# A ViT tower's fusion convolutions: the last 64 channels of both image halves in one 128-partition tile

## The reference

```
dwconv(x, wd, wp, bp): y = depthwise 3x3 (pad 1) of x with wd;  return 1x1 conv of y with wp, + bp
loc  = dwconv(gelu(patch_conv(x)), pl_dw, pl_pw, pl_pwb)
g    = gelu(dwconv(gelu(conv1x1(wavelet_packet(x))), pg_dw, pg_pw, pg_pwb))
glob = conv1x1(g, pg_w2, pg_b2)
h = (1 - gate) * loc + gate * glob              # gate = 0.5 * (tanh(alpha) + 1), per channel
h = relu(dwconv(h, f1)); h = relu(dwconv(h, f2)); h = dwconv(loc + h, f3)
tokens = layernorm(h over the 192 channels) * ln_g + ln_b, and a class token
```

## Time and profile before

| | us |
|---|---|
| median of 3 runs | 229.34 (228.66 to 230.13) |
| profiled execution | 229.1 |
| its span | 227.2 |
| mean granted TensorE clock | 0.852 |

### The profile page before, as it was taken

The page is one execution under the profiler, slowest core; times in us unless marked ns, Lnnn a source line. Parts: engine busy times, 40 slices in busy tenths (PEclk is TensorE's granted clock), DMA queues, the critical chain, the costliest instruction groups (busy, mean ns, idle before and its releaser), DMA issues.

```text
span 227.2 us, 2861 instructions
## 1 busy us (share of the span) xinstructions
PE 161.9 (71%) x928; PEld 133.6 (59%) x928; DVE 102.2 (45%) x302; ACT 47.6 (21%) x89; POOL 75.2 (33%) x196
## 2 busy tenths in 40 slices
PE   0999998888888827610212999999999999993000
PEld 0677754455555415610102899999999999992000
DVE  1129994998899494472103122222332222203445
ACT  0353344343111203210000111232111231110000
POOL 1799300000000121027668877882000000004761
PEclk9999999999999965555555699999999999997555
DMA  6990499999990000003265001000000000011222
GB/s 217 331 408 13 116 265 261 250 261 257 272 341 22 0 1 0 0 0 117 82 197 186 0 5 33 18 19 20 17 31 24 17 20 17 17 38 44 77 56 80
DMA packets 14932, 23.46 MB, mean 103 GB/s; under 512 B 1599, under 2 KB 11396, under 8 KB 14790
## 3 DMA queue, kind: packets, MB, share of 16 engines
q1 hardware_dynamic: 12800, 19.80, 29.9%
q0 software_dynamic: 928, 2.09, 3.0%
q10 hardware_dynamic: 1190, 1.38, 1.9%
HBM read 17.96 MB, written 5.31 MB: 102 GB/s over the span
## 4 chain that ended last, share of the span: by engine, by line
PE 65%; DVE 11%; issue 9%; POOL 5%; DVEq 4%; DMA 3%; ACT 1%; POOLq 0%
PE ps L965 20%; PE ps L975 14%; PE ps L814 8%; PE ps L822 7%; PE ps L823 5%; PE ps L868 4%; POOL diag_s L398 4%; DVEq L746 4%; PE ps L802 3%; DMA w1t_s<-in_w1t 2%; DVE conv L570 1%; DVE stats L616 1%; DVE conv L582 1%; POOL rstd L378 1%; DVE zt L647 1%
## 5 line engine op out<-in xcount | busy, mean ns | idle before, releaser
L965 PE MATMUL ps<-conv 128*128 128x128 f32 x384 | 48.2, 285 | 6.9 <-DVE conv L751 6.5
L965 PEld LDWEIGHTS ps<-conv 128*128 128x128 f32 x384 | 47.3, 201 | 7.6 <-issue 6.8
L570 DVE SCALAR_TENSOR_TENSOR conv<-conv,vecs 128x240 f32<-128x240 f32 (+1 forms) x94 | 35.9, 444 | 7.3 <-ACT conv L447 6.8
L975 PE MATMUL ps<-w_s,conv 128*128 x192 | 33.7, 326 | 0.0
L760 DVE COPY arena<-ps 128x192 f32<-128x192 f32 x16 | 5.7, 358 | 57.5 <-PE ps L975 57.5
L975 PEld LDWEIGHTS ps<-w_s,conv 128*128 128x128 f32 x192 | 30.9, 190 | 0.0
L398 POOL DMA_INDIRECT diag_s<-slot_results,slots x10 | 9.6, 961 | 54.9 <-DMA slot_results<-arena 52.1
L378 POOL TENSOR_TENSOR rstd<-var,neghalf 128x2 f32<-128x2 f32 (+1 forms) x6 | 4.8, 807 | 62.9 <-DVE var L622 62.9
L507 ACT COPY conv<-ps 128x256 f32<-128x256 f32 x16 | 6.0, 373 | 82.8 <-PE ps L956 82.8
L751 DVE COPY conv<-w_s 128x1536 f32 x16 | 15.2, 957 | 14.5 <-issue 9.5
L822 PE MATMUL ps<-conv,pw_s 128*128 128x288 f32 (+1 forms) x48 | 17.4, 445 | 5.5 <-DVE conv L582 3.8
(11 more groups left out here) (152 smaller groups left out, 185.8 us busy)
## 6 DMA issues: line engine op xcount, KB each, us to landing
w_s<-in_w SPq DMA_DIRECT2D x8, 576.0 KB, 18.1
w_s<-in_w SPq DMA_DIRECT2D x8, 384.0 KB
slot_rows<-zero SPq DMA_DIRECT2D x1, 2048.0 KB, 22.2
arena<-in_x SPq DMA_DIRECT2D x4, 432.0 KB, 9.6
w_s<-in_w SPq DMA_DIRECT2D x8, 192.0 KB
slot_results<-arena SPq DMA_DIRECT2D x16, 96.0 KB, 1.6
pw_s<-in_pw SPq DMA_DIRECT2D x1, 1152.0 KB, 11.5
arena<-slot_rows SPq DMA_DIRECT2D x1, 1024.0 KB, 7.6
```

The costliest lines, as they stand in the source:

```text
L570: ins = nc.vector.scalar_tensor_tensor(out=o, in0=a, scalar=w, in1=o, op0=ALU.mult, op1=ALU.add)
L965: last = mm(p1_ps[i % 2][:, c * P:(c + 1) * P], w1_cur[:, i % 2, k * F + c * P:k * F + (c + 1) * P], xs[:, i % 2, k * P:(k + 1) * P], star ...
L975: last = mm(y_ps[i % 2], hT[:, i % 2, k * P:(k + 1) * P], w2_flat[:, bass.ds(expert[i] * (FK * D) + k * D, D)], start=(k == 0), stop=(k == ...
```

## The change

- A fusion round no longer has four tiles but three units: (g 0, t 0), a packed tile (t 1) with half 0 on partitions 0 to 63 and half 1 on 64 to 127, and (g 1, t 0). VectorE, and TensorE with its tap sums, do the units one after another. In round 0 the packed tile is done as two units, its lower and its upper half.
- To get half 1's last channels onto the upper partitions, branches(1) writes its output parts to the swapped halves. The 1x1 weights of tile 1 exist in a second version, pwx, with the rows on the other 64 partitions and zeros on the rest, loaded by one more DMA of 384 KB. A zero fill on POOL clears the part of loc that meets zero weights.
- In rounds 1 and 2 TensorE makes the three upper taps of all three units; in round 0 those of the upper half of the packed tile and of (g 1, t 0). The order of TensorE's queue is new.
- Each fusion 1x1 makes its 64-channel part first. The branches' last pair waits for the third output, not the fourth.
- The constant row is computed after fusion(0, 1), into bank 7, and copied after it.

```diff
-PE_HELPS = [(0, 1), (1, 0), (1, 1), (2, 0), (2, 1)]
+UNITS = [(0, 0), (0, 1), (1, 0)]
+UNIT_BANK = (2, 3, 6)
+FIRST_UNITS = [(0, 0, slice(0, P), 5), (1, 0, slice(0, DB), 6), (1, 1, slice(DB, P), 12), (2, 1, slice(0, P), 12)]
+PE_HELPS = [(0, 1), (0, 2), (1, 0), (1, 1), (1, 2), (2, 0), (2, 1), (2, 2)]
...
# SP
             sp.dma_start(pw_s[:], pw).then_inc(d_pw, 16)
+            sp.dma_start(pwx_s[:], pwx).then_inc(d_pwx, 16)
             sp.dma_start(layout_s[:], layout).then_inc(d_misc, 16)
...
# POOL, ahead of the diagonals
+            nc.gpsimd.memset(loc[LO, 1, HPX:NPX], 0.0).then_inc(loc_zero, 1)
...
# ScalarE
             def branches(g):
+                own, other = (LO, HI) if g == 0 else (HI, LO)
+                first, second = px(0), px(1)
...
-                evacuate(n + 2, b + 1, loc[HI, 1, px(g)], HI, ACT.Gelu, vcol("bias2", 1, HI))
+                evacuate(n + 2, b + 1, loc[other, 1, second], other, ACT.Gelu, vcol(bias, k, other))
...
             def fusion(f, g):
-                evacuate(n + 1, b, act_a[:, 0, px(g)], A, fn, vcol("fb", 2 * f))
-                evacuate(n + 2, b + 1, act_a[LO, 1, px(g)], LO, fn, vcol("fb", 2 * f + 1, LO))
+                if f == 2:
+                    evacuate(n + 1, b + 1, act_a[LO, 1, px(g)], LO, fn, vcol("fb", 2 * f + 1, LO))
+                else:
+                    own = LO if g == 0 else HI
+                    evacuate(n + 1, b + 1, act_a[own, 1, px(0)], own, fn, vcol("fb", 2 * f + 1, own))
+                if f == 0 and g == 1:
+                    act.wait_ge(pw_ev, n + 1)
+                    middle_tap(0, 1, A, V["dwf"] + 18, 1)
+                evacuate(n + 2, b, act_a[:, 0, px(g)], A, fn, vcol("fb", 2 * f))
                 if f == 0:
                     act.wait_ge(pw_ev, n + 2)
-                    for t, rows_ in ((0, A), (1, LO)):
-                        middle_tap(g, t, rows_, V["dwf"] + 18)
+                    middle_tap(g, 0, A, V["dwf"] + 18)
...
-            act.wait_ge(attn_mm, 1)
-            nc.scalar.copy(attn[:], ps[:, 3, 0:D]).then_inc(attn_rdy, 1)
             branches(0)
             branches(1)
             for f in range(3):
                 for g in range(2):
                     fusion(f, g)
+                if f == 0:
+                    act.wait_ge(attn_mm, 1)
+                    nc.scalar.copy(attn[:], ps[:, 7, 0:D]).then_inc(attn_rdy, 1)
...
# VectorE, in place of the loop over f and g
+            for k, (u, ready, rows_, evacuated) in enumerate(FIRST_UNITS):
+                g, t = UNITS[u]
+                c = slice(g * HPX, (g + 1) * HPX)
+                dve.wait_ge(pw_ev, evacuated)
+                nc.vector.scalar_tensor_tensor(out=act_a[rows_, t, c], in0=loc[rows_, t, c],
+                                               scalar=gate[rows_, t:t + 1], in1=glob[rows_, t, c],
+                                               op0=ALU.mult, op1=ALU.add).then_inc(mixed, 1)
+                dve.wait_ge(mixed, k + 1)
+                depthwise(act_a, act_b, V["dwf"], [(g, t, rows_)],
+                          PE_HELPS.index((0, u)) if ready else None, None, UNIT_BANK[u])
+            for f in (1, 2):
+                for u, (g, t) in enumerate(UNITS):
...
+                    dve.wait_ge(pw_ev, 12 + 4 * (f - 1) + (2, 3, 4)[u])
                     if f == 2:
+                        nc.vector.tensor_tensor(glob[:, t, c], act_a[:, t, c], loc[:, t, c],
+                                                ALU.add).then_inc(mixed, 1)
+                        dve.wait_ge(mixed, 4 + u + 1)
+                    src, dst = (act_a, glob)[f - 1], act_b
+                    depthwise(src, dst, V["dwf"] + 18 * f, [(g, t, A)],
+                              PE_HELPS.index((f, u)) if (f, u) in PE_HELPS else None,
+                              6 + u if f == 1 else None, UNIT_BANK[u], f % 2 if t else None)
...
# TensorE
             def branches(g):
...
-                pe.wait_ge(pw_ev, 6 * g + 4)
                 if g == 0:
-                    pe.wait_ge(attn_rdy, 1)
-                pointwise(2, loc, g, b + 2, 2, MA, A)
-                pointwise(2, loc, g, b + 3, 2, MB, LO)
+                    pe.wait_ge(loc_zero, 1)
+                else:
+                    pe.wait_ge(d_pwx, 16)
+                w = pw_s[:, 2, 1] if g == 0 else pwx_s[:, 0]
+                pe.wait_ge(pw_ev, 6 * g + 3)
+                pointwise(2, loc[:, 2, c], loc[:, 1, px(1)], w, b + 2, MA, A)
+                pointwise(2, loc[:, 2, c], loc[:, 1, px(1)], w, b + 3, MB, own)
             def fusion(f, g):
...
-                pe.wait_ge(dw_done, 6 + 4 * f + 2 * g + 2)
-                pointwise(3 + f, src, g, b, 0, MA, A)
-                pointwise(3 + f, src, g, b + 1, 0, MB, LO)
+                own = LO if g == 0 or f == 2 else HI
+                w = pw_s[:, 3 + f, 1] if g == 0 else pwx_s[:, 1 + f]
+                pe.wait_ge(dw_done, 6 + (g + 3 if f == 0 else 4 + 3 * (f - 1) + g + 2))
+                pointwise(3 + f, act_b[:, 0, c], act_b[:, 1, px(f % 2)], w, b + 1, MB, own)
+                pointwise(3 + f, act_b[:, 0, c], act_b[:, 1, px(f % 2)], w, b, MA, A)
+            def taps(f, u):
+                if (f, u) not in PE_HELPS:
+                    return
                 if f == 0:
-                    pe.wait_ge(mixed, 2 * g + 2)
+                    pe.wait_ge(mixed, u + 2)
                 elif f == 1:
-                    pe.wait_ge(pw_ev, 12 + 2 * g + 2)
+                    pe.wait_ge(pw_ev, 12 + (2, 3, 4)[u])
                 else:
-                    pe.wait_ge(mixed, 4 + 2 * g + 2)
+                    pe.wait_ge(mixed, 4 + u + 1)
...
+            def shared_row():
+                pe.wait_ge(d_proj, 32)
+                pe.wait_ge(zeroed, 2)
+                mm(ps[:, 7, 0:D], zero[:, 0:P], proj_s[:, 0, :], start=True, stop=False)
+                mm(ps[:, 7, 0:D], zero[LO, 0:P], proj_s[LO, 1, :], start=False, stop=False)
+                mm(ps[:, 7, 0:D], ones[:], projb_s[:], start=False, stop=True).then_inc(attn_mm, 1)
...
             branches(0)
             branches(1)
+            taps(0, 0)
             for f in range(3):
-                for g in range(2):
-                    if (f, g) in PE_HELPS:
-                        taps(f, g)
-                    fusion(f, g)
+                taps(f, 1)
+                taps(f, 2)
+                fusion(f, 0)
+                if f < 2:
+                    taps(f + 1, 0)
+                fusion(f, 1)
+                if f == 0:
+                    shared_row()
```

More of the change, by code:

```diff
@@ L60, with tower @@
 NROUTE = R_VALID + NT * E
-def tower(nc, x, vec, rows, had, w1t, plw, pw, projw, cls, ident, layout, route, w1, b1, w2, b2, outw, xd, yd, out):
+def tower(nc, x, vec, rows, had, w1t, plw, pw, pwx, projw, cls, ident, layout, route, w1, b1, w2, b2, outw, xd, yd, out):
     with ExitStack() as ctx:
@@ L463, in branches @@
                 evacuate(n + 5, b + 2, glob[:, 0, px(g)], A, ACT.Identity, gate[:, 6:7], gate[:, 2:3])
-                evacuate(n + 6, b + 3, glob[LO, 1, px(g)], LO, ACT.Identity, gate[LO, 7:8], gate[LO, 3:4])
+                evacuate(n + 6, b + 3, glob[own, 1, first], own, ACT.Identity, gate[own, 7:8], gate[own, 3:4])
             def fusion(f, g):
@@ L543, in _, with depthwise @@
                                     ALU.mult).then_inc(gates, 1)
-            def depthwise(src, dst, taps, tiles, help_at=None, mid=None):
+            def depthwise(src, dst, taps, tiles, help_at=None, mid=None, bank=None, to=None):
                 mark = {}
@@ L826, in _, with px @@
             MA, MB = slice(0, P), slice(P, D)
+            def px(g):
+                return slice(g * HPX, (g + 1) * HPX)
             def branches(g):
-                b = 4 * g
+                b, c = 4 * g, px(g)
+                own, other = (LO, HI) if g == 0 else (HI, LO)
                 pe.wait_ge(dw_done, 3 * g + 3)
-                pointwise(1, act_b, g, b + 2, 2, MA, A)
-                pointwise(1, act_b, g, b + 1, 2, MB, HI)
-                pointwise(0, act_b, g, b, 0, MA, A)
-                pointwise(0, act_b, g, b + 1, 0, MB, LO)
@@ L836, in branches @@
[L836 to L851 removed]
+                pointwise(1, act_b[:, 2, c], act_b[:, 1, c], pw_s[:, 1, 1], b + 2, MA, A)
@@ new lines, in branches @@
+                pointwise(1, act_b[:, 2, c], act_b[:, 1, c], pw_s[:, 1, 1], b + 1, MB, other)
+                pointwise(0, act_b[:, 0, c], act_b[:, 1, c], pw_s[:, 0, 1], b, MA, A)
+                pointwise(0, act_b[:, 0, c], act_b[:, 1, c], pw_s[:, 0, 1], b + 1, MB, own)
+                if g == 0:
+                    pe.wait_ge(loc_zero, 1)
[3 more added lines that the diff above has]
+                pe.wait_ge(pw_ev, 6 * g + 3)
@@ L875, in _ @@
             embed_half(1)
-            pe.wait_ge(d_proj, 32)
-            pe.wait_ge(zeroed, 2)
-            mm(ps[:, 3, 0:D], zero[:, 0:P], proj_s[:, 0, :], start=True, stop=False)
-            mm(ps[:, 3, 0:D], zero[LO, 0:P], proj_s[LO, 1, :], start=False, stop=False)
```

(16 more changed lines are left out.)

70 lines of the change are left out of this document (25 added, 45 removed).

## The result

Beside four runs of the kernel before on the same chip (median 229.22 us, 228.66 to 230.13), the changed kernel took 234.14 us (median of 4, 232.48 to 234.90): a ratio of 1.020, with an interval of 1.013 to 1.027. The forecast was 232.9. The profiled execution took 233.56, with a span of 231.7 against 227.2 and a mean granted clock of 0.838 against 0.852.

The account below looks back on a forecast made before the run. The bound alternates between VectorE and TensorE over the fusion rounds, and everything after hangs on their end. Median 229.34, plus 1.75 for order and dependency, plus 1.8 for one clock fall, gives 232.9 us; range 230.0 to 236.0.

Parts of the forecast that it names:

- The clock's term: TensorE idles 2.6 and 2.4 us in round 0, so its clock falls once to half speed: +1.8 us, chance 0.35.
- rival B: The clock falls twice, again in round 2 around TensorE's idle 70.0 to 72.3: another 2.7 us, 235.6, chance 0.22.
- Start: Before the fusion, moved constant row and fewer outputs awaited: VectorE's first mix at 36.2 against 38.70, a gain of 2.5 us.
- Round 0: First fusion round: four units, each alone, 4.69 us without TensorE's help, 3.8 with; end at 53.2 against 52.07 before.
- the first unseen price: VectorE's add waits for a just-ended tap through two semaphores: 0 to 0.15 us each, 0.05 taken.
- Round 0 to 1: fusion(0,0) stands behind taps(0,2) in TensorE's queue, so VectorE idles 1.4 us and next starts at 54.6.
- Constant row: In round 1 the moved row (1.46 us) precedes taps(1,1); the middle unit's add waits to 60.5, round 2 starts at 64.6.
- Order and dependency together: Whole new schedule up to VectorE's first token instruction, clock undisturbed: 1.75 us later, at 79.2 to 79.3.
- POOL's fill, the new weight load, the moved copy: Extra zero fill, 384 KB load on SP's queue and 0.3 us ScalarE copy all fall into waiting or slack: nothing.
- Rival C: Chained taps cost 0.36 us like interleaved ones, not 0.48, so fewer units pay: 228.0, chance 0.10.
- Rival A: Same schedule with the clock holding at 2.4 GHz through the new gaps: 231.1, own range 230.4 to 231.9, chance 0.33.

Follow-up runs that it names:

- e1: The changed kernel with four extra products, results never read, in each of TensorE's three long idle times (two in round 0, one in round 2); 230.61 us, 1.0061.
- e4: e1 with fusion(0,0) put ahead of taps(0,2) in TensorE's queue in round 0; 229.11 us, 1.0014.
- e5: e1 with the constant row computed between branches(1) and the fusion, in place of three of the four extra products there; 229.77 us, 1.0044.
- e3: e1 with the first two units of round 0 done in turn, tap by tap, after both outputs; 230.03 us, 1.0024.
- e2: The changed kernel with extra unread products only in TensorE's two idle times of round 0, the one in round 2 left; 233.12 us, 1.020.
- e7: The kernel before, pairs kept, with only the constant row moved behind branches(1) and the branch outputs put in another order; 226.68 us, 0.9879.
- e6: The edits of e3, e4 and e5 together on the changed kernel, TensorE's gaps filled with extra products; 227.23 us, 0.9937.
- e10: e7 with seven unread products of 256 columns while TensorE waits for the experts' numbers; 223.77 us, 0.9743.
- e8: e6 without any extra product; nine runs from 226.80 to 234.13 us, median 229.2.
- e9: The kernel before with the two tiles of a half done one after another instead of in turn, nothing packed; 249.58 us against 229.78.
- e12: e9 with four unread products of 256 columns ahead of each of the six fusion 1x1 steps; 239.35 us, 1.0462.

## Why the prediction came out right

Its direction and its reasons for the order held. The clock's term was half of what was measured, and in part it was luck that the number came as near as it did. One fall of the clock had been forecast, with a chance of 0.35; what the trace shows is rival B's two, which had 0.22. The stretch grew by 5.40 where 1.75 + 1.8 = 3.55 had been put, and a second miss took half of that error away: the shift was to reach the end of the program whole, and 0.9 us of it did not, 0.8 of that because the first expert products got their clock back sooner. The median came to 234.14 against 232.9.

- *Start.* Forecast 36.2, measured 36.29 for the first mix. The constant row and the handshake were worth 2.4 of the 2.5 us put on them.
- *Round 0.* Four chained units ending at 53.2; measured 53.50. The units without help took 4.70 and 4.73 (4.69 put), those with help 3.91 and 3.87 (3.8 put). The add starts 0.1 after the last tap ends where 0.08 had been put: the first unseen price is real and small.
- *Round 0 to 1.* An idle time of 1.4 on VectorE at an undisturbed clock; e1 shows 1.54, and e4 shows that it was this order alone.
- *Constant row.* Put ahead of taps(1,1), it delays the middle unit and the output ahead of round 2; e5 prices that at 0.64.
- *Order and dependency together.* +1.75 forecast, +1.86 measured by e1's stretch. (By the differences that the prediction said it used, 79.2 to 79.3 less its own 77.6, the forecast would have been 1.6 to 1.7; the conclusion is the same.)
- *POOL's fill, the new weight load, the moved copy.* Put at nothing: the last patch product ended at 29.18 in both traces, and the row's first reader on VectorE follows round 2's last add without idle time, at 77.71.
- *Rival C* (a chained tap costs 0.36) is out: 3.83 for eight. e3 makes the same work 1.78 shorter by doing two units in turn. The rule of the Trainium skill that stood beside it (VectorE: DVE Perf Modes, The DRAIN you can't avoid) compares copies with and without a semaphore between them. No run here makes that comparison, since every tap waits for a semaphore in both orders, so the rule is neither confirmed nor refuted. What counted here is another thing: an operation of another tile between two that depend on each other saved a quarter of the time.
- *The clock* is the term that was mis-sized. The forecast took one fall at 1.8. The first fall came where it was put and cost 1.9. But in the profiled execution there was a second one in round 2, which was rival B's place, at 1.6 and not at the 2.7 put on it, because the clock was back at 78.1 and only half of the last products ran at 1.2 GHz. Together 3.54. The 233.56 of that execution is B in its mechanism and lies between the forecast (232.9) and B (235.6) in its size.
- *Rival A* (the clock holds, 231.1) is what e1 measures: 230.61. The kernel after never ran so fast in its four runs. Its argument, that a gap of up to 2.6 us had been borne, does not hold as a rule: behind 2.37 us in round 2 the clock fell in the kernel after and not in e2.

What stays open: whether a packed tile can pay on top of e7's order. From first mix to first token instruction e6, which has it, takes 39.00 us and e7, which has not, 38.53, so as the units stand here it doesn't; the two together were not tried. Nor do the traces tell why a gap of the same length is followed by a fall in one execution and not in another.

## What to carry to other kernels

Before two tiles are done one after another, look at whether they now run in turn on an engine whose operations depend on each other: here that hid a quarter of each tap. When an order changes, ask of each product in TensorE's queue what stands in front of it that it doesn't need (1.6 us here), and how long TensorE now stands still, because a gap off the path can still cost 1.6 to 1.9 us in clock. If it can't be closed, products that nobody reads are a cheap cover (3.5 us in e1, 2.9 in e10).

## What the runs showed of the hardware beyond that

- Two parts of 64 output columns whose results go to different halves of the partitions, neighbours in the queue, ran together: 1.13 us for both against 1.11 for one. The Trainium skill (TensorEngine Tiling (Array Packing), Tiling Modes) names 128×64 as two independent tiles, and this trace agrees. It takes nothing but the order in the queue, and the kernels before and after both have a part of 128 columns between them.
- The granted clock fell to 0.5 within idle times of 1.81 and 2.38 us (e8), 0.2 us behind one of 2.37 us and 1.1 us behind one of 2.78 us (after). It was still 1.0 behind one of 2.37 us in e2. The runs of one kernel (e8) lie up to 7.3 us apart, the slower ones with the lower mean clock.
- e9's falls cost 3.7 to 12 us beside the 10 of the order, where the whole edit had been put at some 6: at 1.2 GHz the tap sums come late, and VectorE's first add of a half waits up to 4.43 us for them, against 1.42 in e12. TensorE's own waits for VectorE didn't grow by it; they are 2.05 to 2.49 us in e9.
